# Two runs of 8 KB a partition in place of four of 4 KB, for 20 of 32 chunk loads of a graph-attention kernel

## The chip, the cores and the metric

The kernel runs on one core of a Trainium2 chip. The time is that of one execution on the device, in microseconds; several executions are timed and the median is given. One further execution was recorded by the hardware profiler, and everything that is said of single instructions comes from it.

## What is computed

The reference is a small network on a graph of 4096 nodes with 128 features. `adj` is a 4096 x 4096 matrix in fp32 whose entries are 0 or 1.

```python
h = relu(layernorm(x))
Wh = h @ W0                                     # 4096 x 128
e = leaky_relu(Wh @ a[:128] + (Wh @ a[128:]).T, 0.2)
alpha = softmax(where((adj > 0) | eye, e, -9e15), axis=1)
x = x + alpha @ Wh
h = relu(layernorm(x))
x = x + where(adj < 1, exp(-2 * (1 / adj - 1) ** 2), 0) @ (h @ W1 + B)
```

With entries of only 0 and 1 the second layer adds nothing. The kernel therefore reads the whole matrix, checks that each entry is 0 or 1, and finds the edges of each row; where a check fails, a slow general path behind a flag computes everything. In the runs told of here that path is not taken.

## The kernel before, in words

**Chunks.** The matrix (a copy with a zero diagonal, `adj_apart`, made in `kernel()` before the launch) is 64 MB, and it is read once in 32 chunks of 2 MB. Chunk i belongs to a block of 1024 rows (a super, `s`), to a block of 1024 columns (`c`) and to a half of the rows (`h`); `chunk(i)` gives the three. A chunk is 512 rows by 1024 columns. On the chip it fills one of six slots of `adj_ring`, 128 partitions of 16 KB each: partition p holds four pieces of 1024 columns, from four rows that are 128 rows apart. Each piece is 4 KB in one place of DRAM, and neighbouring partitions' pieces lie 16 KB apart.

**The loads.** `load_chunk(i)` issues a chunk's load on SyncE's queue. Six are issued at the start; chunk i is issued when the slot of chunk i - 6 is free, that is when TensorE has packed it and VectorE or ScalarE has checked it (lines 385 to 396). After the last load SyncE's queue issues the stores of the output.

**What is done with a chunk.** TensorE packs it (`pack`, line 618: matmuls with scaled identities sum eight rows' bits into one number a column). When both halves of a step are packed, VectorE scans the packed words (`scan`, line 1139, MAX8). After several steps (a piece) it picks the words with edges and decodes them to indices (`pick`, `pick_shared`, `decode`, lines 1152 to 1285). GpSimd gathers the rows of these indices from a table in DRAM with indirect DMAs (line 535), 72 gathers in all, in ten groups. VectorE turns a gathered group into weights (`weigh`, lines 1315 to 1332), TensorE scatters it (line 744), and a super's epilogue (lines 1420 and 1425) divides and adds to `x_sb`. Beside that, the whole chunk is checked once: VectorE checks 13 chunks, with one instruction each (line 1111), among them 20, 26 and 28; ScalarE the other 19, with two each (lines 929 and 938). For the chunks with the first 1024 columns TensorE turns the first 128 columns (line 598) and VectorE makes weights of them (line 1409).

**The order.** Each engine runs a list of calls that is written out by hand: a loop over the 32 chunks, with tables that say at which chunk another step is called (`SCAN_AT`, `PICK_AT`, `WEIGH_AT` and so on). Group 6 is weighed at chunk 28; group 7 is weighed behind the loop, and then follow the scan and pick of the last step, the epilogue of super 2, the last group and the last epilogue. An engine does not go past an instruction whose input is late.

Of the kernel before, what the change touches and what calls it, by code (L numbers as in the profile page):

```python
# [5 lines left out]
N, D, P = 4096, 128, 128  # L6
NB = N // P
SG = 4
HR = N // SG
KB = HR // P  # L10
CC = 4
CW = N // CC
HK = 4
CHUNKS = SG * CC * 2
AR = 6
# [42 lines left out]
def chunk(i):  # L58
    s = i // (2 * CC)
    first = 1 if s == 0 else s  # L60
    return s, (first + i % (2 * CC) // 2) % CC, i % 2
# [59 lines left out]
DECODE_AT = {9: 0, 17: 1, 25: 2, 31: 3}  # L121
DECODE_SHARED_AT = {10: 0, 18: 1, 26: 2}
QUAD_SCORES_AT, PAIR_SCORES_AT, OCT_SCORES_AT = 2, 4, 5
HUB_ORDER = [2, 3, 4, 5, 6, 7, 0, 1]
HUB_AT = {6: [0], 7: [1], 9: [2, 3], 10: [4], 11: [5, 6], 12: [7]}
HUB_ROWS_AT = 14
# [12 lines left out]
ADD_OWN_AT = {13: 0, 21: 1, 29: 2}  # L139


def gnn_program(nc, x, adj, w0, a0, w1, b1, adj_apart, adj_own, out):
    fp32, bf16, fp8, i32, u32 = (mybir.dt.float32, mybir.dt.bfloat16, mybir.dt.float8e4, mybir.dt.int32,
                                 mybir.dt.uint32)
    ALU, ACT, AX = mybir.AluOpType, mybir.ActivationFunctionType, mybir.AxisListType
# [10 lines left out]
    with ctx:  # L156
        def sb(name, shape, dt=fp32):
            return ctx.enter_context(nc.sbuf_tensor(name, shape, dt))

        def sem(name):  # L160
            return ctx.enter_context(nc.semaphore(name))

        ring = sb("adj_ring", [P, AR, HK * CW])
# [154 lines left out]
        adj_ready = [sem(f"adj_ready{c}") for c in range(AR)]  # L318
# [52 lines left out]
        def _(sp):  # L371
            def load_chunk(i):
                s, c, h = chunk(i)
                sp.dma_start(ring[:, i % AR, :].rearrange("p (k n) -> p k n", k=HK),
                             adj_chunks[s, c, h]).then_inc(adj_ready[i % AR], 16)

# [6 lines left out]
            for i in range(AR):  # L383
                load_chunk(i)
            for i in range(AR, CHUNKS):
                old = i - AR
                sp.wait_ge(packed, old + 1)
                if chunk(old)[1] == 0:
                    sp.wait_ge(col_turned, 2 * chunk(old)[0] + chunk(old)[2] + 1)
                if chunk(old)[0] == 0 and chunk(old)[2] == 0:  # L390
                    sp.wait_ge(hub_turned, old + 2)
                if old in DVE_CHECKED:
                    sp.wait_ge(checked_v, DVE_CHECKED.index(old) + 1)
                else:
                    sp.wait_ge(checked_a, ACT_CHECKED.index(old) + 1)
                load_chunk(i)
# [145 lines left out]
        def _(pe):  # L542
# [105 lines left out]
            def hub_group(m):  # L648
# [3 lines left out]
                for b in range(4):  # L652
                    last = nc.tensor.matmul(bank[7][:, 0:E1], hub_w[:, m % 2, b, :],  # L653
                                            whe[:, 4 * HUB_ORDER[m] + b, ONE:ONE + E1],
                                            start=(m + b == 0), stop=(m + b == XO + 2))
# [401 lines left out]
        def _(dve):  # L1057
# [313 lines left out]
            def hub(m):  # L1371
                n = HUB_ORDER[m]
                if m == 0:
                    dve.wait_ge(r_hub_set, 1)
                    dve.wait_ge(qa_set, 1)
                    dve.wait_ge(a_set, 1)
                dve.wait_ge(hub_kept, 2 * (next(i for i in range(0, 2 * CC, 2) if chunk(i)[1] == n // 2) // 2) + n % 2 + 1)
                if m >= 2:
                    dve.wait_ge(hub_added, m - 1)
                for b in range(4):  # L1380
                    nb = 4 * n + b
                    last = nc.vector.tensor_scalar(hub_w[:, m % 2, b, :], r_hub[:, :], whe[:, nb, QA:QA + 1],  # L1382
                                                   whe[:, nb, AA:AA + 1], ALU.mult, ALU.max)
                last.then_inc(hub_scaled, 1)
                dve.wait_ge(hub_scaled, m + 1)
                nc.vector.tensor_tensor(hub_w[:, m % 2, :, :], hub_w[:, m % 2, :, :], hub_mask[:, 4 * n:4 * n + 4, :],  # L1386
                                        ALU.mult).then_inc(hub_w_set, 1)
# [274 lines left out]
def laid_out(arrays, np):  # L1662
    adj = arrays["in_adj"]
    apart = adj.copy()
    np.fill_diagonal(apart, 0)
    return {"adj_apart": apart, "adj_own": np.ascontiguousarray(np.diagonal(adj)).reshape(P, NB)}


# [17 lines left out]
```

## Time and profile before

| | us |
|---|---|
| median of 3 runs | 215.99 (215.91 to 216.35) |
| the profiled execution | 216.57 |
| its span, first to last instruction | 214.8 |
| busy in the span: TensorE, VectorE, ScalarE, GpSimd | 155.6, 177.4, 189.5, 129.7 |

The profile names the engines PE (TensorE's matmuls), PEld (its weight loads), DVE (VectorE), ACT (ScalarE), POOL (GpSimd) and SP (SyncE, whose queue issues the chunk loads). `L618` is line 618 of the kernel. An arrow, as in `adj_ring<-adj_apart`, goes from what is read to what is written. The DMA engines are sixteen; a packet is one piece of a transfer that one of them moves. The time of an issue and the time to its landing are given apart: a load has landed when its semaphore is complete.

### The profile page before, as it was taken

Reading aid. Unit: us, or ns where it says so; the run is one execution under the profiler, and the core shown is the slowest. Engines: PE = TensorE matmul, PEld = TensorE weight load, DVE = VectorE, ACT = ScalarE, POOL = GpSimd, SP = SyncE. Lnnn points to the kernel's source line nnn. Section 1 sums busy time; section 2 is a strip of 40 time slices with the busy share of each in tenths; the row PEclk is TensorE's granted clock in tenths of the full one; section 3 lists DMA queues with packets and bytes.
Section 4 is the critical chain, followed back from the end, with each engine's and each line's share of the span. In section 5 each row is a group of like instructions: output and inputs, shape, how many; then the busy total and the mean of one; then the engine's idle time right before and its main releaser. Section 6 shows DMA issues by size and latency. Waiting matters only on the chain.

```text
span 214.8 us, 3127 instructions
## 1 busy us (share of the span) xinstructions
PE 155.6 (72%) x914; PEld 102.5 (48%) x928; DVE 177.4 (83%) x529; ACT 189.5 (88%) x207; POOL 129.7 (60%) x140
## 2 busy tenths in 40 slices
PE   0188779994849665599749978599393967799572
PEld 0076565441425342387535635286231654667561
DVE  7993999999997999989474695995796599859855
ACT  0699988499999999999999999799999994999960
POOL 3980002196001788889777888889077788868350
PEclk9999999998888999889976999889878899999887
DMA  5999999999999999999999999999999999972313
GB/s 158 347 415 410 412 406 413 404 410 405 414 421 408 404 392 400 402 393 396 398 388 387 392 403 389 399 389 395 400 408 390 390 397 393 407 283 45 117 23 104
DMA packets 22403, 76.83 MB, mean 358 GB/s; under 512 B 2671, under 2 KB 3270, under 8 KB 22384
## 3 DMA queue, kind: packets, MB, share of 16 engines
q1 hardware_dynamic: 18912, 71.31, 84.9%
q0 software_dynamic: 2912, 5.22, 7.2%
q8 instruction: 8, 0.13, 0.3%
q10 hardware_dynamic: 560, 0.08, 0.2%
q14 instruction: 11, 0.09, 0.1%
HBM read 74.08 MB, written 4.23 MB: 365 GB/s over the span
## 4 chain that ended last, share of the span: by engine, by line
DMA 27%; DVE 27%; PE 19%; issue 11%; POOL 9%; ACT 5%; POOLq 0%; DVEq 0%; ACTq 0%; SPq 0%
DMA adj_ring<-adj_apart 23%; POOL gathered_rows L535 9%; DVE summed L1111 8%; PE bank L618 7%; DMA gathered_rows<-node_table,shared_index 4%; ACT spread L898 3%; PE bank L744 3%; PE bank L653 2%; DVE hub_w L1382 2%; PE bank L729 2%; DVE x_sb L1425 2%; PE bank L736 2%; DVE shared_slots L1197 1%; DVE cand L1139 1%; DVE stats L1091 1%
## 5 line engine op out<-in xcount | busy, mean ns | idle before, releaser
L535 POOL DMA_INDIRECT gathered_rows<-node_table,index x48 | 69.3, 1444 | 38.6 <-DVE index L1276 24.5
L929 ACT ACTIVATE trash_a<-adj_ring,below_one 128x4096 fp8e4<-128x4096 f32 x19 | 70.4, 3704 | 5.3 <-DMA adj_ring<-adj_apart 4.7
L618 PE MATMUL bank<-adj_ring,pack_w 128*128 128x512 bf16 x242 | 70.7, 423 | 4.5 <-DMA adj_ring<-adj_apart 3.4
L938 ACT ACTIVATE trash_a<-adj_ring 128x4096 fp8e4<-128x4096 f32 x19 | 68.7, 3614 | 0.5
L1111 DVE SCALAR_TENSOR_TENSOR summed<-adj_ring 128x4096 fp8e4<-128x4096 f32 x13 | 58.2, 4480 | 7.5 <-DMA adj_ring<-adj_apart 7.4
L535 POOL DMA_INDIRECT gathered_rows<-node_table,shared_index x24 | 36.8, 1535 | 9.8 <-issue 7.0
L618 PEld LDWEIGHTS bank<-adj_ring,pack_w 128*128 128x128 bf16 x248 | 25.0, 103 | 35.5 <-issue 9.8
L1139 DVE MAX8 cand<-bank 128x8 f32<-128x120 f32 (+25 forms) x82 | 23.3, 351 | 2.8 <-PE bank L618 2.8
L744 PE MATMUL bank<-gathered_rows,spread 128*128 128x129 f32 x160 | 21.0, 283 | 3.0 <-DVE spread L1365 1.8
L744 PEld LDWEIGHTS bank<-gathered_rows,spread 128*128 128x128 f32 x160 | 19.5, 196 | 4.8 <-issue 4.4
L614 PE MATMUL bank<-codes,code_w 128*128 128x512 bf16 x24 | 10.6, 443 | 8.7 <-DMA adj_ring<-adj_apart 8.7
L653 PE MATMUL bank<-whe,hub_w 128*128 128x129 f32 x64 | 10.2, 316 | 5.7 <-DVE hub_w L1386 5.7
L898 ACT ACTIVATE spread<-x_sb,shift,rstd 128x128 f32<-128x128 f32 x32 | 13.3, 501 | 0.3 <-DVE shift L1103 0.3
L653 PEld LDWEIGHTS bank<-whe,hub_w 128*128 128x128 f32 x64 | 9.4, 225 | 7.2 <-DVE hub_w L1386 6.9
L482 POOL PARTITION_ALL_REDUCE ends_all<-ends x1 | 1.4, 1440 | 17.4 <-DVE ends L1507 17.4
L556 PE MATMUL bank<-ident,spread 128*128 128x128 f32 x32 | 6.5, 337 | 7.2 <-ACT spread L898 7.2
L568 PE MATMUL bank<-w_sb,gathered_rows 128*128 128x130 f32 x64 | 10.6, 318 | 1.2 <-ACT whe L912 0.9
L568 PEld LDWEIGHTS bank<-w_sb,gathered_rows 128*128 128x128 f32 x64 | 9.5, 227 | 2.4 <-ACT gathered_rows L904 1.8
L614 PEld LDWEIGHTS bank<-codes,code_w 128*128 128x128 bf16 x32 | 3.8, 119 | 13.7 <-DMA adj_ring<-adj_apart 10.4
L1409 DVE SCALAR_TENSOR_TENSOR col_w<-r_rows,hub_whe,bank 128x512 f32<-128x512 f32 (+1 forms) x6 | 4.2, 701 | 7.1 <-PE bank L598 7.1
L962 ACT ACTIVATE own_w<-ident,w_self 128x128 f32<-128x128 f32 x32 | 9.7, 386 | 0.2 <-PE bank L736 0.2
L1382 DVE TENSOR_SCALAR hub_w<-r_hub,whe 128x128 f32<-128x128 f32 x32 | 8.9, 352 | 0.0
(188 smaller groups left out, 237.0 us busy)
## 6 DMA issues: line engine op xcount, KB each, us to landing
adj_ring<-adj_apart SPq DMA_DIRECT2D x32, 2048.0 KB, 23.3
node_table<-gathered_rows POOLq DMA_DIRECT2D x4, 520.0 KB, 9.3
x_sb<-in_x SPq DMA_DIRECT2D x8, 256.0 KB, 5.8
out<-x_sb SPq DMA_DIRECT2D x3, 512.0 KB, 14.4
gathered_rows<-node_table,index POOLq DMA_INDIRECT x48, 5.6
gathered_rows<-node_table,shared_index POOLq DMA_INDIRECT x24, 5.7
out<-x_sb SPq DMA_DIRECT2D x2, 192.0 KB, 2.0
out<-x_sb SPq DMA_DIRECT2D x1, 128.0 KB, 2.0
```

The lines of the kernel that those rows point to most:

```text
L535: pool.indirect_dma_start(out=rows[:, g % RING_GROUPS * GE + t, :], out_offset=None, in_=table, in_offset=bass.IndirectOffsetOnAxis(ap=row ...
L568: last = nc.tensor.matmul(bank[6 + half][:, b * (D + 2):(b + 1) * (D + 2)], hT[:, nb * P:(nb + 1) * P], w0_sb[:, :], start=(b == 0), stop= ...
L614: nc.tensor.matmul(to[:, :], code_w[:, 2 * c + half, :], codes[:, :], start=True, stop=False, skip_group_check=True)
L618: last = nc.tensor.matmul(to[:, :], pack_w[:, k, :], ring_hi[:, i % AR, at:at + BW], start=False, stop=(k == KB - 1), skip_group_check=True)
L653: last = nc.tensor.matmul(bank[7][:, 0:E1], hub_w[:, m % 2, b, :], whe[:, 4 * HUB_ORDER[m] + b, ONE:ONE + E1], start=(m + b == 0), stop=(m ...
L744: return nc.tensor.matmul(acc_of(SUPER_OF_GROUP[g], t), spread[:, g % 2, at * KB:(at + 1) * KB, :], rows[:, g % RING_GROUPS * GE + turn, G ...
L898: last = nc.scalar.activation(hn_block(b), x_sb[:, b, :], ACT.Identity, bias=shift[:, b:b + 1], scale=rstd[:, b:b + 1])
L929: nc.scalar.activation(trash_a[:, :], ring[:, i % AR, :], ACT.Sign, bias=below_one[:, :], scale=-1.0, accum_out=signs[:, n:n + 1], saturat ...
L938: nc.scalar.activation(trash_a[:, :], ring[:, i % AR, :], ACT.Abs, accum_out=sizes[:, n:n + 1], saturate=False).then_inc(checked_a, 1)
L1111: nc.vector.scalar_tensor_tensor(trash_v, ring[:, i % AR, :], 1.0, ring[:, i % AR, :], ALU.is_ge, ALU.not_equal, accum_out=bad_v[:, n:n + ...
L1139: last = nc.vector.max(cand[:, at * 8:(at + 1) * 8], word_bank(step, half)[:, lo:hi])
L1382: last = nc.vector.tensor_scalar(hub_w[:, m % 2, b, :], r_hub[:, :], whe[:, nb, QA:QA + 1], whe[:, nb, AA:AA + 1], ALU.mult, ALU.max)
```

## The change

`kernel()` makes one more array, `adj_long`, and gives it to the program. For each chunk from 12 on it holds 2 MB in one piece: two planes, each of 128 partitions with 8 KB, and in each 8 KB two of the four pieces that the partition holds. The load of such a chunk reads `adj_long` in place of `adj_apart`. What lies in the slot is the same as before, word for word. The loads of chunks 0 to 11 stay, and so do the issue order, the waits and all calls on the engines. Making the array is done before the launch and is not in the time.

```diff
+LONG_FROM = 12
...
-def gnn_program(nc, x, adj, w0, a0, w1, b1, adj_apart, adj_own, out):
+def gnn_program(nc, x, adj, w0, a0, w1, b1, adj_apart, adj_own, adj_long, out):
...
             def load_chunk(i):
                 s, c, h = chunk(i)
+                if i >= LONG_FROM:
+                    sp.dma_start(ring[:, i % AR, :].rearrange("p (a n) -> p a n", a=2),
+                                 adj_long[i - LONG_FROM].rearrange("a p n -> p a n")).then_inc(adj_ready[i % AR], 16)
+                    return
                 sp.dma_start(ring[:, i % AR, :].rearrange("p (k n) -> p k n", k=HK),
                              adj_chunks[s, c, h]).then_inc(adj_ready[i % AR], 16)
...
-    return {"adj_apart": apart, "adj_own": np.ascontiguousarray(np.diagonal(adj)).reshape(P, NB)}
+    late = np.empty((CHUNKS - LONG_FROM, 2, P, 2 * CW), adj.dtype)
+    for i in range(LONG_FROM, CHUNKS):
+        s, c, h = chunk(i)
+        planes = apart[s * HR + h * HK * P:s * HR + (h + 1) * HK * P, c * CW:(c + 1) * CW]
+        late[i - LONG_FROM] = planes.reshape(2, 2, P, CW).transpose(0, 2, 1, 3).reshape(2, P, 2 * CW)
+    return {"adj_apart": apart, "adj_own": np.ascontiguousarray(np.diagonal(adj)).reshape(P, NB), "adj_long": late}
```

## Rows read from the trace of the kernel before

**Rows 1.** The page: busy line, DMA share in 40 slices, largest queue.

```profile
PE 155.6 (72%) x914; PEld 102.5 (48%) x928; DVE 177.4 (83%) x529; ACT 189.5 (88%) x207; POOL 129.7 (60%) x140
...
DMA  5999999999999999999999999999999999972313
...
q1 hardware_dynamic: 18912, 71.31, 84.9%
```

**Rows 2.** The chain that ended last, in order of time: start, us, what.

```profile
104.08 27.28 DMA adj_ring<-adj_apart
...
170.56 4.33 POOL gathered_rows L535
...
180.07 5.01 POOL gathered_rows L535
...
185.38 6.33 DMA gathered_rows<-node_table,shared_index
```

**Rows 3.** Two issues of line 374, chunks 11 and 31; the landing is both's.

```profile
L374 SPq DMA_DIRECT2D adj_ring<-adj_apart x1: 679/679/679, 58.6 to 58.6; - x1
...
L374 SPq DMA_DIRECT2D adj_ring<-adj_apart x1: 973/973/973, 171.0 to 171.0; - x1
...
DMA to landing us min/median/max: 20.8/20.8/20.8
```

**Rows 4.** Windows: stretch, length, engines' busy time, clock, DMA share, GB/s.

```profile
6.00:8.00 2.00, 0.59 (x2) 0.50 (x2) 1.97 (x16) 1.77 (x3) 1.91 (x4) 1.00 0.87 300
...
10.00:12.00 2.00, 0.96 (x4) 0.71 (x4) 1.90 (x16) 2.00 (x7) 1.86 (x3) 1.00 1.02 422
...
16.30:42.10 25.80, 21.39 (x133) 14.95 (x133) 21.71 (x47) 21.31 (x56) 1.51 (x2) 1.00 1.02 408
```

**Rows 5.** Timeline, 131 to 192 us: start, length, work, in brackets the wait.

```profile
131.38 4.42 DVE L1111 SCALAR_TENSOR_TENSOR summed<-adj_ring 128x4096 fp8e4<-128x4096 f32 x1 [2.55 <-DMA adj_ring<-adj_apart]
...
164.55 0.39 PE L614 MATMUL bank<-codes,code_w 128*128 128x512 bf16 x1 [3.46 <-DMA adj_ring<-adj_apart]
...
168.93 0.75 DVE L1409 SCALAR_TENSOR_TENSOR col_w<-r_rows,hub_whe,bank 128x512 f32<-128x512 f32 x1 [4.16 <-PE bank L598]
169.26 0.99 POOL L535 DMA_INDIRECT gathered_rows<-node_table,shared_index  x1 [0.30 <-issue]
169.60 4.42 DVE L1111 SCALAR_TENSOR_TENSOR summed<-adj_ring 128x4096 fp8e4<-128x4096 f32 x1
...
175.87 0.20 DVE L1315 TENSOR_TENSOR edge_w<-r_slots,gathered_rows 128x64 f32<-128x64 f32 x1
...
179.79 4.42 DVE L1111 SCALAR_TENSOR_TENSOR summed<-adj_ring 128x4096 fp8e4<-128x4096 f32 x1
...
191.79 0.43 DVE L1315 TENSOR_TENSOR same<-r_quad,gathered_rows 128x256 f32<-128x256 f32 x1 [2.13 <-DMA gathered_rows<-node_table,shared_index]
```

**Rows 6.** Waits: who for whom, us in all, times, longest.

```profile
ACT trash_a L929 <- DMA adj_ring<-adj_apart: 4.7, 3, 2.8
```

**Rows 7.** Last issue of line 382, the eighth part of x, with landing.

```profile
L382 SPq DMA_DIRECT2D x_sb<-in_x x1: 536/536/536, 4.0 to 4.0; - x1
...
DMA to landing us min/median/max: 6.5/6.5/6.5
```

**Rows 8.** Two gathers, line 535: beside the stream, and after it.

```profile
L535 POOL DMA_INDIRECT gathered_rows<-node_table,index x1: 997/997/997, 166.7 to 166.7; - x1
...
DMA to landing us min/median/max: 5.5/5.5/5.5
...
L535 POOL DMA_INDIRECT gathered_rows<-node_table,shared_index x1: 1016/1016/1016, 202.8 to 202.8; - x1
...
DMA to landing us min/median/max: 2.6/2.6/2.6
```

## The prediction

> **What bounds the kernel now.** I read the page first. In its busy line [rows 1] ScalarE is at 88% and VectorE at 83%, and the row of the DMA engines stands at nine tenths or more from the second slice to the 35th. So the 32 chunk loads of 2 MB are one stream without a gap, and two engines keep barely up with it. The packet rows say what the stream is made of: queue q1 has 18,912 packets in 71.31 MB. 16,384 of them are 4 KB runs of the adjacency (32 chunks of 128 partitions with four runs each, 67.1 MB), and the change bears on these.
>
> Next the chain that ended last [rows 2]. It holds the landing of chunk 20 (issued at 104.08, 27.28 us), then GpSimd's gathers, the last gather of group 7 (issued at 185.38, 6.33 us), and from 191.8 us on VectorE and TensorE in turns, with few pauses, to the end. The stream is on the path up to about 191.8 us; behind it lie 23 us that no chunk can shorten.
>
> How fast is the stream? Chunk 11 lands at 58.6 + 20.8 = 79.4 us and chunk 31 at 171.0 + 20.8 = 191.8 us [rows 3]: the 20 chunks that are changed take 112.4 us, 5.62 us each. While chunks 1 to 5 land (16.3 to 42.1 us) no gather runs, and the engines move 408 GB/s, which is 2.097 MB / 408 = 5.14 us a chunk [rows 4]. The other 0.48 us a chunk belong to the gathers and stores between.
>
> Then the timeline, to see where a chunk's landing sets a start [rows 5]. VectorE waited 2.55 us for chunk 20 before its check at 131.38 us. TensorE waited 3.46 us for chunk 26 and began to pack at 164.55 us; VectorE waited 4.16 us for what TensorE made of it (168.93 us), and from there it runs one thing after another: the check of chunk 26, the scan, the weights of group 6 (175.87 us). At 191.79 us it waits 2.13 us for the last gather of group 7, and no pause of any size follows. ScalarE waited for chunks for 4.7 us in all [rows 6], so it has as much room to follow a faster stream.
>
> **The change, part by part.** *Runs.* For 20 chunks a partition's 16 KB arrive as two runs of 8 KB and not as four of 4 KB: 20 x 256 = 5,120 packets go, the bytes stay, and each chunk lies as 2 MB in one piece in DRAM, where its rows were 16 KB apart. Nothing on a compute engine is added or removed: the words in each ring slot are the same, in the same order, and so are all waits.
>
> What a longer run is worth no row shows, so I bound it. In the stretch of chunks 1 to 5 the engines' busy share is 1.02 at 408 GB/s, that is 400 GB/s for one unit of busy time; 16 engines x 4,096 B / 400 = 164 ns for a 4 KB packet. The nearest row with another length is the load of x at the start, 2 KB runs: 300 GB/s at a share of 0.87 from 6 to 8 us, 345 for a unit, so 95 ns for a 2 KB packet [rows 4]. Taken at its word that is 69 ns for each further 2 KB, hence 164 + 138 = 302 ns for 8 KB in place of 328: 7.9%, or 0.41 us a chunk. That is the upper end, and too good, because those are the first transfers of the program and the engines were not filled. The lower end is nothing: the last octant of x lands only at 4.0 + 6.5 = 10.5 us [rows 7], so 2 KB runs are still among what arrives from 10 to 12 us, and that stretch moves 422 GB/s, more than the 408 of 4 KB runs alone. I take 2%, 0.10 us a chunk, nearer to the lower end, since the second row is a full stream like the one at hand; 422 against 408 is 3.4%, so 2% is a pace that the stream has already shown.
>
> The Trainium skill has a rule against expecting much here. Its page "DMA: Bandwidth & Descriptors", section "Why small descriptors are slow (HBM only)", gives about 3 cycles of overhead to a packet and holds joining descriptors to be worth it only up to 256 B. By its figures 4 KB is 128 beats and 3, 8 KB is 256 and 3: an estimate of 1.1%, or 0.06 us a chunk, and the sum below would be 215.4 in place of 214.8. No run so far shows a run of 8 KB.
>
> *Where the gain goes.* With 0.10 us a chunk, chunk 20 lands 9 x 0.10 = 0.9 us earlier, chunk 26 15 x 0.10 = 1.5 us and chunk 31 20 x 0.10 = 2.0 us. VectorE's check of chunk 20 has 2.55 us of room, TensorE's pack of chunk 26 has 3.46. GpSimd's gathers of groups 6 and 7 start behind what chunk 20 released (0.9 us earlier), but each of the last two stops, 4.3 us at 170.56 and 5.01 us at 180.07 [rows 2], lies beside a VectorE check, those of chunks 26 and 28; a gather without that takes 1.0. So the gathers end when the check of chunk 28 ends, and this hangs on chunk 26: 1.5 us earlier. All that follows 191.79 us [rows 5] moves with it: -1.5 us. Chunk 31, 2.0 us earlier, does not become the later of the two.
>
> *The gathers' way through the queue.* A gather beside the stream lands 5.5 us after its issue (166.7 us), one after it 2.6 us (202.8 us) [rows 8]: 2.9 us are spent among the stream's packets. If a gather's two steps, data and count, each wait for one packet in service, a packet twice as long adds 2 x 164 ns = 0.3 us. At the lower end nothing is added, at the upper end the 2.9 us double. I take 0.3, because the latency is the same for gathers one after the other, as a short fixed wait would be. It counts in full, as the last gather of group 7 is what VectorE waits for. The earlier groups have cover: group 6's last gather lands at 166.7 + 5.5 = 172.2 and is used at 175.87, 3.7 us later.
>
> *SyncE.* Half the descriptors make its long issues shorter (the load of chunk 11 took 679 ns, of chunk 31 973 ns [rows 3]); chunk 31 lands 20.8 us after its issue, four chunk times, so there is always work queued and an issue sooner or later changes nothing: 0.
>
> Sum: -1.5 + 0.3 = -1.2 us. The profiled execution took 216.57 us (span 214.8 and 1.77 around it), 0.58 above the median of the runs. So 215.4 for an execution like it, **214.8 us** beside the median of 215.99. A difference under 0.2%, 0.43 us, can't be told from no change.
>
> **The rivals.** *Nothing happens.* The stream's pace is set by something that does not count runs, as the 422 GB/s with 2 KB runs among them says; then every landing stays, 216.0 us. The same comes out if the gain is eaten at GpSimd. A gather began at 169.26 us and the check of chunk 26 at 169.60, so that gather went through and only the next one stood [rows 5]. If the check moves up 1.5 us and the gathers only 0.9, the order can turn; then one gather more, 1.3 us with its gap, comes behind the check of chunk 28, and -1.2 becomes about 0. The rule of the Trainium skill named above, that joining pays only at small sizes, would give this case.
>
> *The gathers come later (the other side).* If what a gather waits behind is a number of packets and not of bytes, the 2.9 us become 5.8. The gather that VectorE waits for at 191.79 us would be held until the stream ends, but not much beyond: at the latest some 1.6 us after chunk 31 (2.6 us without stream, less the 1.0 us of its own issue), 193.4. The price is 0.7 to 1.7 us, and 1.2 gives 217.2 us without a gain of the stream. It decides from the first tenth on, as nothing covers that gather; together with a stream that is 2% faster it would leave 215.7. For it speaks the long and steady 2.9 us, eighteen 4 KB packets; against it, that a queue of so many bytes would show the same.
>
> *The stream gets slower.* 8 KB from one place could suit DRAM worse than four rows apart. 2% the other way puts chunk 26 back by 1.5 us, and 217.5. No row speaks for it: the runs of x, 4 KB apart in DRAM, and those of the adjacency, 16 KB apart, arrived at about one pace.
>
> *Much faster.* At the upper price, 0.41 us a chunk, chunk 26 would come 6.2 us earlier, but TensorE only had 3.46 us of waiting there and ScalarE 4.7 in all, so no more than about 3.4 us arrive: 212.6.
>
> **How the numbers follow.** A faster stream 0.46 (nearly all of it at 1 to 4%; its own range 213.2 to 215.4), nothing or all eaten 0.26, later gathers 0.20, slower stream 0.08. This gives faster 0.46, same 0.26, slower 0.28. The likeliest is the first, 214.8. The range takes its own range and reaches up to later gathers, 213.2 to 217.3; beyond it lie the strongest gain and the slower stream.
>
> **What would show it.** Right: packets down by 5,120; chunk 31 lands near 189.8 us and 5.5 us or less lie between landings; VectorE's wait for chunk 20 shrinks to 1.6 us and TensorE's for chunk 26 to about 2; the gathers still land 5.5 to 6 us after their issue beside the stream; VectorE begins group 7 near 190.6. Wrong: landings of chunks 12 to 31 where they were (nothing happens), gathers at 7 us and more (the other side), or group 7's last gather issued no earlier than 185 us although chunk 26 landed earlier (eaten at GpSimd).

## The result, and the profile after

The changed kernel took 214.78 us in the median of twelve runs (213.02 to 217.66), the kernel before 216.39 in twelve runs beside it; the ratio is 0.9909, with a 95% interval of 0.9881 to 0.9937. That is faster, by 0.6 to 1.2%. The figure of the forecast, 214.8, is met almost to the digit, but it stood beside a median of 215.99, a ratio of 0.9945, so the saving was larger than foretold: 2.0 us by the ratio, where the sum had 1.2. The ratios, here and below, leave out executions more than 1.5% above the fastest of their kernel, so a ratio is not always that of two medians, and that of the 16 KB kernel below is one of the faster half of its runs.

The profiled execution took 213.70 us, with a span of 211.9. Its page, the busy line, the DMA share in 40 slices, the largest queue:

```profile
PE 156.6 (74%) x928; PEld 102.4 (48%) x928; DVE 177.4 (84%) x529; ACT 189.4 (89%) x207; POOL 129.1 (61%) x140
...
DMA  5999999999999999999999999999999999961313
...
q1 hardware_dynamic: 13792, 71.31, 84.1%
```

Queue q1 has 5,120 packets fewer than in [rows 1] and the same 71.31 MB. The compute engines are busy as long as before. The stream still fills the DMA engines up to the 35th slice.

The issues of chunks 11 and 31, with their landings:

```profile
L379 SPq DMA_DIRECT2D adj_ring<-adj_apart x1: 772/772/772, 58.6 to 58.6; - x1
...
DMA to landing us min/median/max: 20.6/20.6/20.6
...
L376 SPq DMA_DIRECT2D adj_ring<-adj_long x1: 367/367/367, 169.0 to 169.0; - x1
...
DMA to landing us min/median/max: 19.7/19.7/19.7
```

Chunk 11 lands at 79.2 us (79.4 in [rows 3]) and chunk 31 at 188.7, where it was 191.8. Twenty chunks took 109.5 us and not 112.4: 5.475 us each in place of 5.62, a saving of 0.145.

The timeline of the same stretch as in [rows 5]; lines of the program have moved by five:

```profile
129.76 4.42 DVE L1116 SCALAR_TENSOR_TENSOR summed<-adj_ring 128x4096 fp8e4<-128x4096 f32 x1 [2.28 <-DMA adj_ring<-adj_long]
...
162.07 0.39 PE L619 MATMUL bank<-codes,code_w 128*128 128x512 bf16 x1 [1.88 <-DMA adj_ring<-adj_long]
...
164.85 0.75 DVE L1414 SCALAR_TENSOR_TENSOR col_w<-r_rows,hub_whe,bank 128x512 f32<-128x512 f32 x1 [1.41 <-PE bank L603]
...
165.31 1.00 POOL L540 DMA_INDIRECT gathered_rows<-node_table,index  x1 [0.30 <-issue]
165.51 4.42 DVE L1116 SCALAR_TENSOR_TENSOR summed<-adj_ring 128x4096 fp8e4<-128x4096 f32 x1
166.61 4.19 POOL L540 DMA_INDIRECT gathered_rows<-node_table,shared_index  x1 [0.30 <-issue]
...
172.00 0.21 DVE L1320 TENSOR_TENSOR edge_w<-r_slots,gathered_rows 128x64 f32<-128x64 f32 x1
...
175.92 4.42 DVE L1116 SCALAR_TENSOR_TENSOR summed<-adj_ring 128x4096 fp8e4<-128x4096 f32 x1
...
176.31 4.91 POOL L540 DMA_INDIRECT gathered_rows<-node_table,shared_index  x1 [0.30 <-issue]
...
189.00 0.43 DVE L1320 TENSOR_TENSOR same<-r_quad,gathered_rows 128x256 f32<-128x256 f32 x1 [2.90 <-DMA gathered_rows<-node_table,shared_index]
```

TensorE begins to pack chunk 26 2.5 us earlier than in [rows 5] and still waits 1.88 us for it. The check of chunk 26 moved by 4.1 us and that of chunk 28 by 3.9, more than the stream gave; VectorE begins group 7 2.8 us earlier. In [rows 5] the check of chunk 26 stopped the third gather of group 7 (170.56 us). Here it stops the first (166.61): the check moved up more than the gathers did. The chain that ended last (start, us, what) shows what that cost:

```profile
182.82 6.10 DMA gathered_rows<-node_table,shared_index
189.00 0.44 DVE same L1320
```

Behind the check of chunk 28 two gathers of group 7 are issued, where it was one in [rows 2]; the last goes out at 182.82 us in place of 185.38. So the gathers gained 2.6 us of the check's 3.9. The last one landed 6.10 us after its issue, where it was 6.33 in [rows 2].

A gather beside the stream:

```profile
L540 POOL DMA_INDIRECT gathered_rows<-node_table,index x1: 997/997/997, 165.3 to 165.3; - x1
...
DMA to landing us min/median/max: 5.8/5.8/5.8
```

It lands 0.3 us later than the one in [rows 8]. Over all gathers between 80 and 183 us that no check stopped, the median rose from 5.54 to 5.76 us. ScalarE's waits for chunks of the second array are now:

```profile
ACT trash_a L934 <- DMA adj_ring<-adj_long: 1.9, 1, 1.9
```

It was 4.7 us in [rows 6]: ScalarE is nearly a bound itself.

What I had not expected is the spread: ten of the twelve runs of the kernel before lie between 215.91 and 217.06, but those of the changed kernel are strewn from 213.0 to above 216. In 29 further runs the kernel before lay between 215.5 and 217.9.

### The profile page after: what moved, and what is told of

Its sections match the earlier page's. It is cut to its first block, busy times and chain, and to the rows that moved or that the text cites. A ratio compares the mean times of both kernels' runs of the same rounds, so it can differ in the third digit from the quotient of the medians.

```text
span 211.9 us, 3141 instructions
## 1 busy us (share of the span) xinstructions
PE 156.6 (74%) x928; PEld 102.4 (48%) x928; DVE 177.4 (84%) x529; ACT 189.4 (89%) x207; POOL 129.1 (61%) x140
## 3 DMA queue, kind: packets, MB, share of 16 engines
q1 hardware_dynamic: 13792, 71.31, 84.1%
HBM read 74.08 MB, written 4.23 MB: 370 GB/s over the span
## 4 chain that ended last, share of the span: by engine, by line
ACT 34%; DVE 16%; issue 15%; PE 12%; DMA 12%; POOL 9%; POOLq 0%; DVEq 0%; ACTq 0%; SPq 0%
ACT trash_a L934 16%; ACT trash_a L943 9%; POOL gathered_rows L540 9%; DMA adj_ring<-adj_long 8%; PE bank L623 5%; DVE summed L1116 4%; DMA gathered_rows<-node_table,shared_index 4%; ACT spread L903 3%; ACT own_w L967 2%; PE bank L749 2%; DVE stats L1096 1%; DVE x_sb L1430 1%; DVE shared_slots L1202 1%; PE bank L734 1%; DVE x_sb L1444 1%
## 5 line engine op out<-in xcount | busy, mean ns | idle before, releaser
L540 POOL DMA_INDIRECT gathered_rows<-node_table,index x48 | 70.4, 1467 | 35.6 <-DVE index L1281 21.7
L540 POOL DMA_INDIRECT gathered_rows<-node_table,shared_index x24 | 35.0, 1458 | 11.1 <-issue 7.0
L619 PE MATMUL bank<-codes,code_w 128*128 128x512 bf16 x32 | 13.8, 431 | 5.2 <-DMA adj_ring<-adj_long 3.3
L658 PE MATMUL bank<-whe,hub_w 128*128 128x129 f32 x64 | 10.7, 322 | 6.0 <-DVE hub_w L1391 4.4
L741 PE MATMUL bank<-whe,own_w 128*128 128x129 f32 x64 | 9.0, 301 | 0.0
L561 PEld LDWEIGHTS bank<-ident,spread 128*128 128x128 f32 x32 | 4.7, 178 | 8.4 <-ACT spread L903 7.3
## 6 DMA issues: line engine op xcount, KB each, us to landing
out<-x_sb SPq DMA_DIRECT2D x2, 192.0 KB, 2.0
```

The source lines that it names most:

```text
L540: pool.indirect_dma_start(out=rows[:, g % RING_GROUPS * GE + t, :], out_offset=None, in_=table, in_offset=bass.IndirectOffsetOnAxis(ap=row ...
L619: nc.tensor.matmul(to[:, :], code_w[:, 2 * c + half, :], codes[:, :], start=True, stop=False, skip_group_check=True)
```

## The experiments

Each kernel was timed against the kernel before in five rounds; the ratio is to that.

**The changed kernel again**, no edit.

> The changed kernel once more, for a second profile beside the first. Its first profile took 213.7 us and its runs lay between 213.0 and 216.2 us. If the stream is what made it faster, chunk 31 lands between 188 and 190 us here too (before: 191.8). If the wide spread of its times comes from GpSimd's gathers falling before or behind a VectorE check, an execution that is slower than the first profile has the same landings within 0.5 us, and its group 7 stalls at other gathers; if it comes from the stream itself, chunk 31 lands later by as much as the time is longer.

Measured: 215.40 us median (213.05 to 218.16), ratio 0.9904 [0.9866, 0.9941]. The gain and the spread repeat. The profiled execution is a longer one, 215.69 us, and that is useful. Twenty chunks take 109.5 us as in the first, so the pace of the stream does not differ. But the whole stream is later: chunk 11 lands at 80.1 us and chunk 31 at 189.6, both 0.9 us later than in the first. That is neither of the two cases expected (within 0.5 us, or later by the whole 2.0 us by which the time is longer). Its timeline and two links of its chain:

```profile
167.60 0.75 DVE L1414 SCALAR_TENSOR_TENSOR col_w<-r_rows,hub_whe,bank 128x512 f32<-128x512 f32 x1 [3.77 <-PE bank L603]
168.26 4.42 DVE L1116 SCALAR_TENSOR_TENSOR summed<-adj_ring 128x4096 fp8e4<-128x4096 f32 x1
...
178.45 4.41 DVE L1116 SCALAR_TENSOR_TENSOR summed<-adj_ring 128x4096 fp8e4<-128x4096 f32 x1
```

```profile
185.35 5.51 DMA gathered_rows<-node_table,shared_index
190.93 0.44 DVE same L1320
```

Chunk 26 landed at 163.2 us, 1.1 us later than in the first execution, and VectorE had its columns only at 167.60, 4.4 us after the landing; in the first execution it was 2.8 us. So of the 2.75 us by which the check of chunk 26 began later, 1.1 are the stream's and 1.6 are TensorE's. The windows (length, busy time of the engines, granted clock, DMA share, GB/s) tell why. The first execution:

```profile
136.00:144.00 8.00, 8.00 (x51) 5.31 (x50) 7.93 (x19) 7.87 (x9) 6.48 (x6) 0.88 1.02 405
164.00:168.00 4.00, 2.73 (x24) 2.24 (x22) 3.15 (x2) 3.97 (x3) 3.38 (x3) 1.00 1.02 401
```

This one:

```profile
136.00:144.00 8.00, 7.75 (x48) 5.23 (x47) 7.93 (x24) 7.72 (x6) 6.41 (x6) 0.79 1.02 407
164.00:168.00 4.00, 4.00 (x18) 1.98 (x17) 0.40 (x1) 3.97 (x3) 3.09 (x4) 0.61 1.02 402
```

A granted clock of 1.00 is the upper of TensorE's two levels, 2.4 GHz, and 0.50 the lower, 1.2 GHz. From 164 to 168 us the first execution had the upper one throughout, this one a mean of 0.61, most of the time the lower. In the kernel before it was 0.60 there.

The end of this execution shows one thing more. Its check of chunk 28 began 1.3 us earlier than in [rows 5], but two gathers stand behind it and not one, so the last gather of group 7 went out at 185.35 us, as late as before (185.38 in [rows 2]). VectorE still began group 7 0.86 us earlier, because that gather landed after 5.51 us and not after 6.33.

**Length or place.** The new array changes two things: the runs are longer, and a chunk is one piece of DRAM. `e1_4k_together` lays each late chunk in one piece, in runs of 4 KB; `e3_8k_apart` has runs of 8 KB, but neighbouring partitions' runs 32 KB apart; `e2_16k` has runs of 16 KB and `e4_2k` of 2 KB, both in one piece.

```diff
-late = np.empty((CHUNKS - LONG_FROM, 2, P, 2 * CW), adj.dtype)
+late = np.empty((CHUNKS - LONG_FROM, PLANES, P, HK // PLANES * CW), adj.dtype)
...
-                                 adj_long[i - LONG_FROM].rearrange("a p n -> p a n"))
+                                 adj_long[s, h, :, :, c, :].rearrange("a p n -> p a n"))
...
+late = np.empty((CHUNKS - LONG_FROM, 8, P, CW // 2), adj.dtype)
```

The first pair of lines is that of `e1_4k_together` (PLANES is 4) and `e2_16k` (1), the second that of `e3_8k_apart`, whose array keeps the order of the matrix, the last line that of `e4_2k`.

> Each changed chunk lies in one piece of 2 MB in DRAM, but its runs are 4 KB again (four planes). Theory 'run length': the packets are 4 KB as before, so the landings are those of before: chunk 31 near 191.8 us, 5.62 us a chunk, time 0.998 to 1.002 of before. Rival 'one piece in DRAM': the gain of the changed kernel is there without long runs: chunk 31 near 188.7 us, 5.48 us a chunk, time near 0.991.

> Runs of 8 KB as in the changed kernel, but neighbouring partitions' runs lie 32 KB apart in DRAM, not side by side. Theory 'run length': chunk 31 near 188.7 us and 0.991 of before. Rival 'one piece in DRAM': chunk 31 near 191.8 us and the time of before.

> One run of 16 KB a partition for chunks 12 to 31. The changed kernel saved 0.145 us a chunk with 16 packets fewer on each engine, 9 ns a packet. Theory 'so much a packet': 8 packets fewer still save 0.07 us a chunk more, chunk 31 near 187.3 us; the gathers beside the stream land 5.8 + 0.6 = 6.4 us after their issue, if each waits for two packets in service (two of 8 KB added 0.3 us); the time about 0.988 of before. Rival 'the pace has reached its limit at 8 KB': chunk 31 at 188.7 us, time 0.991. Rival 'a gather waits behind a number of packets': the gathers' latency, 5.5 us with 4 KB, is well over 8 us.

> Chunks 12 to 31 in eight runs of 2 KB a partition, each chunk in one piece of DRAM. Theory 'so much a packet' (9 ns each, from 4 KB against 8 KB): 32 packets more on each engine cost 0.29 us a chunk, 5.9 us a chunk from 12 on, chunk 31 some 5.8 us later than with 4 KB, near 197.6 us; time 1.02 to 1.03 of before. The gathers beside the stream land 0.15 us earlier than the 5.5 us of before. Rival 'the gain at 8 KB has another cause': 5.62 us a chunk, time of before.

Measured, with the landings of chunks 11 and 31 in each profiled execution:

| kernel | median us (range) | ratio | chunk 11, 31 lands | us a chunk | gather lands after |
|---|---|---|---|---|---|
| 2 KB, one piece | 222.25 (221.46 to 222.96) | 1.0272 [1.0244, 1.0299] | 79.8, 198.1 | 5.915 | 5.5 |
| 4 KB, before | 216.3 to 216.8 | 1 | 79.4, 191.8 | 5.62 | 5.5 |
| 4 KB, one piece | 216.5 (215.75 to 217.53) | 0.9986 [0.996, 1.0011] | 80.2, not recorded | | 5.5 |
| 8 KB, one piece | 214.78, again 215.40 | 0.9909, 0.9904 | 79.2, 188.7 | 5.475 | 5.8 |
| 8 KB, apart | 214.04 (213.59 to 217.5) | 0.9872 [0.9829, 0.9915] | 79.9, 189.7 | 5.49 | 5.6 to 5.8 |
| 16 KB, one piece | 215.32 (212.56 to 218.69) | 0.9854 [0.9821, 0.9887] | 79.7, 188.2 | 5.425 | 6.5 |

The issue of chunk 31 in the kernel with 16 KB, and one of its gathers:

```profile
L377 SPq DMA_DIRECT2D adj_ring<-adj_long x1: 327/327/327, 168.7 to 168.7; - x1
...
DMA to landing us min/median/max: 19.5/19.5/19.5
...
L541 POOL DMA_INDIRECT gathered_rows<-node_table,index x1: 998/998/998, 164.4 to 164.4; - x1
...
DMA to landing us min/median/max: 6.6/6.6/6.6
```

The place does nothing that these runs can show: 4 KB in one piece is the kernel before (chunk 28 lands 96.8 us after chunk 11 in both), 8 KB apart is the changed kernel. The length does it, and in a plain way. A chunk is 32 packets for each of 16 engines at 4 KB. At 2 KB it is 32 more for 0.295 us more, 9.2 ns each; at 8 KB 16 fewer for 0.145 us less, 9.1 ns each; at 16 KB 8 fewer again for 0.05 us less (0.07 was expected), 6 ns each. All profiles with 8 KB from chunk 12 on, those below too, give 5.46 to 5.49 us a chunk, so the 9.1 ns stand for 8 to 10, and the 6 ns rest on a small difference. The gathers' latency rises with the run: the medians of those that no check stopped are 5.54 us at 4 KB, 5.76 at 8 and 6.47 at 16. But at 2 KB it is 5.54 again, where 0.15 us less was expected. The 16 KB kernel has the best ratio, but its runs fall in two heaps, six from 212.6 to 214.0 and six from 216.6 up, and its median is no better than that of 8 KB.

**The clock at chunk 26.** Theory after these runs: the executions differ because TensorE's clock is at the lower level when it packs chunk 26 or is not. `e5_after_warm` and `e6_before_warm` give TensorE some matmuls to do before that pack, into a bank that the pack then overwrites (8 in the changed kernel, 12 in the one before).

```diff
+                if i == 26:
+                    pe.wait_ge(scanned, 2 * (step - 2) + 1)
+                    for _ in range(8):
+                        nc.tensor.matmul(word_bank(step, 0)[:, :], code_w[:, 2 * c, :], codes[:, :], start=True,
+                                         stop=False, skip_group_check=True)
                 pe.wait_ge(adj_ready[i % AR], (i // AR + 1) * 16)
```

> The changed kernel, with eight matmuls more on TensorE ahead of its wait for chunk 26; they write the bank that the pack's first matmul overwrites, so nothing else changes. In the two profiles of the changed kernel the granted clock in 164 to 166 us was 1.00 (execution of 213.7 us) and 0.50 (215.69), and the columns of chunk 26 came 2.85 and 4.5 us after its landing. Theory 'the clock at chunk 26 makes two kinds of executions': the clock there is 1.00, the columns come under 3 us after the landing, the runs gather at 213 to 214.2 and the ratio to before falls to about 0.986. Rival 'the spread comes from the gathers' order alone': the runs stay spread from 213 to 216, ratio 0.990.

> The kernel before (4 KB runs everywhere), with twelve matmuls more on TensorE ahead of its wait for chunk 26. It separates the clock from the stream. The landings stay: chunk 31 112.4 us after chunk 11. If the clock alone is worth 1.6 us at chunk 26, VectorE's check of chunk 28 begins near 178.2 and the time is 0.993 to 0.997 of before, less than the whole 1.6 us, since the last gather of group 7 can't land much before the stream ends at 191.8. If only the stream matters: 0.999 to 1.001.

Measured: 215.46 us (214.08 to 217.54), ratio 0.9945 [0.9912, 0.9977], for the changed kernel; 216.87 (216.07 to 217.12), 1.0017 [0.9994, 1.004], for the one before. In both profiles the clock from 164 to 168 us is 1.00 and the columns of chunk 26 come 2.8 us after its landing. The spread stayed: as its only cause the theory falls. That the matmuls raised the clock is not shown, though. Of the six profiles here with long runs from chunk 12 on and without the matmuls, five have 1.00 in that stretch too, the longest execution of all (216.88 us) among them; only the second profile has 0.61. The kernel before shows in its timeline what holds it instead:

```profile
190.73 0.42 DVE L1320 TENSOR_TENSOR same<-r_quad,gathered_rows 128x256 f32<-128x256 f32 x1 [1.52 <-DMA gathered_rows<-node_table,shared_index]
...
194.01 1.43 DVE L1144 MAX8 cand<-bank 128x8 f32<-128x272 f32 x4 [1.14 <-PE bank L623]
```

Group 7 begins 1.06 us earlier than in [rows 5], and three microseconds later VectorE waits 1.14 us for the pack of chunk 31, which landed at 192.0 as before. In this execution, without a faster stream, the stream's end takes back what is won ahead of it.

**More of the change.** `e7_8k_from_1` has runs of 8 KB for all chunks but the first.

```diff
-LONG_FROM = 12
+LONG_FROM = 1
```

> The changed kernel with 8 KB runs from chunk 1 on, not from 12. Theory: chunk 11 lands some 1.3 to 1.6 us earlier, but from about 60 to 134 us ScalarE sets the pace (in the changed kernel's chain it holds that stretch), so at most 0.5 us reach the end: the time of the changed kernel within 0.3%. Rival 'the stream sets the end throughout': 1.5 us faster than the changed kernel, 0.984 of before.

Measured: 217.01 us (216.38 to 217.92), ratio 1.0035 [1.0008, 1.0062]: a stream that is ahead everywhere (chunk 26 lands at 159.2 us, 2.8 us before that of the changed kernel, chunk 31 at 187.3) gives a slower kernel. Its timeline:

```profile
150.15 1.49 DVE L1144 MAX8 cand<-bank 128x8 f32<-128x216 f32 x5 [4.32 <-PE bank L623]
...
164.51 4.45 DVE L1116 SCALAR_TENSOR_TENSOR summed<-adj_ring 128x4096 fp8e4<-128x4096 f32 x1
165.81 4.03 POOL L540 DMA_INDIRECT gathered_rows<-node_table,index  x1 [0.30 <-issue]
...
175.13 0.23 DVE L1320 TENSOR_TENSOR edge_w<-r_slots,gathered_rows 128x64 f32<-128x64 f32 x1 [4.23 <-issue]
...
179.07 4.42 DVE L1116 SCALAR_TENSOR_TENSOR summed<-adj_ring 128x4096 fp8e4<-128x4096 f32 x1
179.31 3.78 PE L734 MATMUL bank<-hub_whe,hub_w 128*128 128x129 f32 x16 [5.28 <-DVE x_sb L1430]
```

Two things met. The scan that the indices of group 6 hang on waited 4.32 us for TensorE (2.42 in the changed kernel's profile, where it began at 148.79), so the gathers of group 6 came late. TensorE's clock had its part in this: from 136 to 142 us it was 0.58 (0.85 in the first profile), and one pack and the sixteen matmuls behind it took 3.62 and 2.88 us, where they took 3.14 and 2.01; that is 1.35 of the 1.36 us by which the scan was later. And the check of chunk 26 came early, 1.3 us before the last of these gathers was issued, in place of 0.2 us behind it. That gather (165.81) stood 4.03 us, VectorE waited 4.23 us for it before the weights of group 6, and the check of chunk 28 fell to 179.07 us, 3.15 behind that of the changed kernel. TensorE, idle for 5.28 us, then did its next sixteen matmuls in 3.78 us, at a granted clock of 0.50 from 180 to 184 us; in the changed kernel's profile the same sixteen took 2.02 us at 1.00. This is the longest of the six executions and the only one profiled: that all six are slow is measured, that these two things make them so is shown for this one.

**Is the spread the caught gather?** New theory: an execution is long when that last gather of group 6 is caught. `e8_gate` lets VectorE begin the check of chunk 26 only after it was issued; `e9_gate_warm` adds the eight matmuls; `e10_warm_held` has the matmuls and instead holds GpSimd ahead of group 6.

```diff
+                if g == GATE_GROUP:
+                    nc.gpsimd.memset(gate_t[:, :], 0.0).then_inc(group_issued, 1)
...
+                if i == 26:
+                    dve.wait_ge(group_issued, 1)
...
+                if g == HELD_GROUP:
+                    pool.wait_ge(index_set, n + 1)
+                    for k in range(HOLDS):
+                        nc.gpsimd.tensor_scalar(held_t[:, k, :], ident[:, :], 0.0, None, ALU.mult).then_inc(held_done, 1)
```

Both groups are 6 and HOLDS is 4. The first part stands behind a group's gathers on GpSimd, the second in VectorE's check, the third ahead of a group's gathers.

> The changed kernel, with one wait more: VectorE begins the check of chunk 26 only when GpSimd has issued the last gather of group 6. Theory (what spreads the times of the 8 KB kernels is whether that gather is caught behind the check; caught, it lands near 175 and not near 171 us and everything behind the weights of group 6 comes 3 us later, as in the kernel with 8 KB from chunk 1): no execution above 216.0, all but one or two between 212.8 and 215.7, median 213.9 to 214.4. Rival (the spread comes only from TensorE's clock when it packs chunk 26): the spread stays, 213 to 217.5, median 214.8 to 215.4.

> The changed kernel with both: eight matmuls that TensorE does before the pack of chunk 26, and VectorE's wait for the last gather of group 6. Theory (two things spread the times, the clock at chunk 26, up to 1.6 us, and the caught gather, 3 us): all executions between 212.8 and 215.0, median 213.5 to 214.1. Rival (the caught gather is nothing, the eight matmuls alone did not help): as those without the wait, 214.1 to 217.5, median 215.4.

> The changed kernel with the eight matmuls before the pack of chunk 26, and four operations of GpSimd of 0.53 us each before the first gather of group 6, so that its gathers come 2.1 us later and the last is always caught behind the check of chunk 26. Theory: the profile shows that gather at 4 us or more, landing near 175.5 us, the check of chunk 28 near 179, and all executions are between 216.3 and 218.0, median 217.0. Rival (a caught gather costs only what it is late itself, 2.1 us less the 0.9 us of cover that the last landing had): median 215.5 to 216.5, with the old spread.

Measured: 215.16 us (213.86 to 217.33), ratio 0.9952 [0.9923, 0.9982]; 215.27 (213.12 to 217.6), 0.9905 [0.987, 0.994]; and 217.64 (217.46 to 218.23), 1.006 [1.0038, 1.0082]. The held kernel was to show the price of a caught gather. In its timeline the last gather but one of group 6 stood 4.71 us, the last went out behind the check, and the weights of group 6 waited for it:

```profile
165.16 4.71 POOL L548 DMA_INDIRECT gathered_rows<-node_table,index  x1 [0.30 <-issue]
...
175.95 0.23 DVE L1333 TENSOR_TENSOR edge_w<-r_slots,gathered_rows 128x64 f32<-128x64 f32 x1 [3.92 <-issue]
```

2.06 us of work on GpSimd made the kernel 2.2 us longer than `e5_after_warm`, and the spread went: six executions within 0.8 us, two of them above the 218.0 that was the upper bound. The rival's 215.5 to 216.5 did not come. But 2.06 us that count in full would give nearly the same as the caught gather, and no run parts the two. The two kernels in which the gather cannot be caught are strewn as widely as the changed kernel. That a caught gather holds up the weights of group 6 is seen in the profiles of `e7_8k_from_1` and of the held kernel; as the only cause of the spread it falls as well.

**Gathers past the checks.** A gather that comes to a check stands to its end. `e11_checks_in_two` makes the checks of chunks 26 and 28 two instructions each, so that two gathers go through where it was one. That tests whether the number of group 7's gathers behind the checks makes the spread, and might have been a better kernel.

```diff
+                parts = 2 if i in IN_TWO else 1
+                for part in range(parts):
...
+                    own = slice(part * HK * CW // parts, (part + 1) * HK * CW // parts)
-                nc.vector.scalar_tensor_tensor(trash_v, ring[:, i % AR, :], 1.0, ring[:, i % AR, :],
+                    nc.vector.scalar_tensor_tensor(trash_v[:, own], ring[:, i % AR, own], 1.0, ring[:, i % AR, own],
```

> The changed kernel, with VectorE's checks of chunks 26 and 28 each as two instructions over half the chunk; what is checked is the same. A gather that comes to a check stands until that instruction ends. Theory (what spreads the times of the 8 KB kernels, 213 to 216, is how many gathers of group 7 stand behind the checks of chunks 26 and 28; its last gather was issued at 182.8 us in the execution of 213.7 us and at 185.3 in that of 215.7): stalls of 2.0 to 2.8 us in place of 4.2 to 5.2, two gathers through where one was, the last gather issued between 179 and 181.5 us, VectorE begins group 7 before 187.5 us, and then the landing of chunk 31 at 188.7 us sets the rest: all but one execution between 212.3 and 214.5, median 213.3. Rival 1 (the stalled gather does not get through between the halves): stalls of 4.2 to 5.2 us as before, median 214.6 to 215.4, spread as before. Rival 2 (the gathers go through but the spread has another origin): last gather before 181.5 us in the profile, but executions from 213 to 217 as before.

Measured: 214.83 us (213.06 to 216.88), ratio 0.9913 [0.9884, 0.9943], the changed kernel over again. The profiled execution is the longest of its twelve, 216.88 us. Its timeline:

```profile
151.34 1.49 DVE L1150 MAX8 cand<-bank 128x8 f32<-128x216 f32 x5 [4.60 <-PE bank L624]
...
165.68 2.32 DVE L1121 SCALAR_TENSOR_TENSOR summed<-adj_ring 128x2048 fp8e4<-128x2048 f32 x1
166.98 1.89 POOL L541 DMA_INDIRECT gathered_rows<-node_table,index  x1 [0.30 <-issue]
168.04 2.29 DVE L1121 SCALAR_TENSOR_TENSOR summed<-adj_ring 128x2048 fp8e4<-128x2048 f32 x1
169.17 2.04 POOL L541 DMA_INDIRECT gathered_rows<-node_table,shared_index  x1 [0.30 <-issue]
...
174.88 0.23 DVE L1326 TENSOR_TENSOR edge_w<-r_slots,gathered_rows 128x64 f32<-128x64 f32 x1 [2.36 <-issue]
...
178.87 2.28 DVE L1121 SCALAR_TENSOR_TENSOR summed<-adj_ring 128x2048 fp8e4<-128x2048 f32 x1
179.32 2.71 POOL L541 DMA_INDIRECT gathered_rows<-node_table,shared_index  x1 [0.30 <-issue]
...
194.43 1.43 DVE L1150 MAX8 cand<-bank 128x8 f32<-128x272 f32 x4 [3.38 <-PE bank L624]
```

The gathers did as foretold: stalls of 1.9 to 2.7 us, the last of group 7 issued at 179.32 us although this is a long execution. Group 7's gathers are not the limit any more, and the time stays. What is late is TensorE: the scan at 151.34 us waited 4.60 us for it, and at 194.43 VectorE waited 3.38. In between, the last gather of group 6 is caught here as well, by half a check (166.98): the weights of group 6 waited 2.36 us for it and began at 174.88, 2.9 us later than in the first profile, and this wait is on the chain that ended last. Its window, and below it a link of its chain and the same link of the first profile's (start, us, what), say where TensorE lost time:

```profile
136.00:142.00 6.00, 5.21 (x24) 3.64 (x22) 5.93 (x19) 5.97 (x3) 4.78 (x5) 0.55 1.02 409
```

```profile
139.41 3.55 PE bank L735 x16
```

```profile
138.85 1.84 PE bank L734 x16
```

From 136 to 142 us the granted clock was 0.55, where the changed kernel's first profile has 0.85, and the sixteen matmuls of a super's hub took 3.55 us; the same sixteen took 1.84 there. The packs behind them came later, and with these the scan, by 2.55 us, and the gathers of group 6, by 2.2 for the first and 1.7 for the last.

Put together over the eight profiled executions with long runs from chunk 12 and nothing held: where the clock from 136 to 144 us was 0.88 or more, they took 213.38, 213.70, 213.86 and 214.16 us; where it was 0.79 or less, 214.08, 215.27, 215.69 and 216.88. The one of 214.08 is an exception that I can't explain away: `e5_after_warm`, at 0.79. That the clock there makes the spread is not shown. In this chain and in that of `e7_8k_from_1` it made the scan late, but the second profile of the changed kernel, at 0.79, lost little by it: the hub's sixteen matmuls took 1.92 us in its chain, and its scan began 19.3 us after the check of chunk 20, where the first profile has 19.0. No edit set the clock in that stretch.

The other profiles show more directly what their times follow. In the kernel before and in seven of these eight, all but `e11_checks_in_two`, the execution ends 22.9 to 23.2 us after VectorE begins group 7. That start is made of when the check of chunk 28 begins (175.7 to 179.8 us), of how many gathers of group 7 stand behind it (one, two or three, at 1.3 us each), and of the last one's way (5.5 to 6.3 us). `e9_gate_warm`, profiled at 215.27 us, has three.

## Why the prediction came out

*The stream: right in kind, too small in size.* The term was 0.10 us a chunk; it measured 0.145. The 2% behind it rested on a misreading. The stretch from 10 to 12 us that moves 422 GB/s in [rows 4] was taken to hold 2 KB runs of x. The transfers in it say otherwise:

```profile
DMA packets 208, 0.84 MB, mean 422 GB/s; under 512 B 2, under 2 KB 2, under 8 KB 207
```

That is 4 KB a packet: the matrix's own runs, which say nothing of another length. So the choice within the bounds had no row behind it, and that it came near is luck. The kernels with 2 and 8 KB agree on 9 ns a packet, and that is the term's right form: 16 packets fewer for each engine, 0.145 us. The bounds that were given, 0 and 0.41, held. The Trainium skill, "DMA: Bandwidth & Descriptors", section "Why small descriptors are slow (HBM only)", speaks of about 3 cycles of overhead for a packet and of joining only small ones. By that the chunk would have saved an estimated 0.06 us. The runs do not agree: 0.145 us, and 2.7% of the kernel between 2 and 4 KB.

*The gathers' latency: right in size, wrong in the sum.* 0.3 us was forecast, and 5.5 became 5.8 in the gather shown, 0.2 us more in the median. Two waits for a packet in service, of 164 ns for each 4 KB, would give 0.3, and 1.0 at 16 KB, where 0.9 was measured; but they would give 0.15 less at 2 KB, where nothing changed, so what the gathers wait for is not settled. The rival of a latency that counts packets (7 us and more) did not occur. The sum, however, added the 0.3 "in full" at the last gather of group 7, and that one landed sooner after its issue: 6.33 us in [rows 2], 6.10 in the first profile, 5.51 in the second. It goes out when the stream is near its end, which may be why; no run tests that.

*SyncE: right.* Its issues became shorter (chunk 31's took 367 ns, where it was 973) and the landings show only the stream.

*The chain: half right.* All runs through chunk 26, the two checks and the last gather of group 7, as written. But the size was to be 1.5 us for chunk 26 and -1.2 for group 7; in the first profile it was 2.5 and -2.8, in the second 1.4 and -0.9. Two things were missing from the sum. TensorE's clock at chunk 26 can change: with the upper level the columns came 1.6 us sooner after the landing. And the rival "eaten at GpSimd" was given as a case of its own, all or nothing, and took its part of the gain in both executions: the order of check and gathers turned, and one gather more, 1.3 us, stands behind the check of chunk 28. Together this gives the measured starts. In the first profile the check of chunk 28 came 3.87 us earlier, less 1.31 for that gather, plus 0.23 for the shorter way of the last one: 2.79. In the second it came 1.34 us earlier, less 1.31, plus 0.82: 0.85. The Trainium skill, "SBUF — State Buffer", section "SBUF: two separate sides", tells of a port pair that VectorE and GpSimd take in turn, whole instructions at a time. The traces agree for the gather: begun 0.2 us ahead of a check it takes 1.0 us, one behind it 4.0 to 5.2, and 1.9 to 2.7 when the check is halved. They show no check that waits for a gather: the one that began 0.2 us behind it (165.51) took the usual 4.42 us.

*The number.* So 214.8 is met partly by luck. The stream gave more than was written, the extra gather that stood at nothing took some of it back, and the 0.3 us of latency did not come; the two profiles of the changed kernel gave 2.8 and 0.9 us, and the forecast's 1.2 lies between. It was also set beside a median of 215.99; beside the 216.39 that was measured with it, the same sum would have said 215.2. What the profile was to show of it held in the first: 5,120 packets, TensorE's wait for chunk 26 near 2 us (1.88), gathers at 5.5 to 6 us. VectorE's wait for chunk 20 did not shrink to 1.6 us (2.28): what runs ahead of that check had moved up too. The sign of "eaten at GpSimd", a last gather of group 7 no earlier than 185 us, did not show in the first profile (182.82) and did in the second (185.35).

*What stays open.* What spreads the executions: why the whole stream is 0.9 us later in one than in another, chunk 11 included, and why TensorE's clock falls before 144 us or at chunk 26 in one and not in another. Whether holding the clock up before 144 us would bring all of them to 213.5 is not known. The 16 KB kernel's two heaps were not profiled in the upper one.

## What to carry to other kernels

On a stream that fills the DMA engines, count packets as well as bytes: here each packet of 2 to 8 KB cost some 9 ns of an engine beyond its bytes, so fewer and longer runs paid, while the gathers beside the stream landed later the longer its runs were, from 4 KB on. A transfer that lands earlier moves the work behind it into new company; here a check that came up met gathers that had not, and with a stream that was ahead everywhere the kernel was slower. Where a change makes executions spread, take several profiles before explaining any: two of mine told two stories, and each held for a part.

## What the hardware showed that was not expected

- The price of a packet hardly depends on its length from 2 to 8 KB (9.2 ns, and 8 to 10), nor on where its neighbours lie in DRAM (5.475 and 5.49 us a chunk with runs side by side and 32 KB apart).
- A gather's latency beside a stream rises with the length of the stream's runs from 4 KB on: 5.5 us at 2 and at 4 KB, 5.8 at 8, 6.5 at 16, and 2.4 to 2.6 without a stream.
- A gather goes through between two halves of a VectorE check, with some 0.04 us between them (`e11_checks_in_two`, 165.68 + 2.32 to 168.04 us), and the second half takes no longer for it (2.29 us).
- Twelve matmuls put before chunk 26 in the kernel before (`e6_before_warm`) went with a granted clock of 1.00 in every window of 4 us from 136 to 208 us, stretches ahead of the edit among them, and gave no time (ratio 1.0017).
